# Who signals for TensorE: a drain behind each group of matmuls in place of the group's last matmul

## What is computed

```python
src, tgt = x[row], x[col]
h = relu(concatenate([src, tgt, edge_attr], -1) @ W1 + b1)
msg = h @ W2 + b2
attn = sigmoid(concatenate([msg, conf], -1) @ Wa + ba)
out = segment_sum(msg * attn, col, num_segments=100000)
return layernorm(x + out)
```

## Time and profile before

| | us |
|---|---|
| median of the 3 runs shown | 793.27 |
| lowest, highest | 778.97, 797.54 |
| profiled execution, from its first to its last instruction (span) | 792.5 |
| PE matmuls busy | 425.7 |
| DVE busy | 502.9 |
| ACT busy | 427.9 |
| POOL busy | 457.6 |

### The profile page before, as it was taken

The page is one execution under the profiler, slowest core; times in us unless marked ns, Lnnn a source line. Parts: engine busy times, 40 slices in busy tenths (PEclk is TensorE's granted clock), DMA queues, the critical chain, the costliest instruction groups (busy, mean ns, idle before and its releaser), DMA issues. The chain is left out here.

```text
span 792.5 us, 8991 instructions
## 1 busy us (share of the span) xinstructions
PE 425.7 (54%) x1902; PEld 299.8 (38%) x1902; DVE 502.9 (63%) x2146; ACT 427.9 (54%) x1089; POOL 457.6 (58%) x473
## 2 busy tenths in 40 slices
PE   1842778463764136763646566656463475543560
PEld 0531545332543123643435254444251254322250
DVE  5944988878793228883667579888461995330542
ACT  0433686678963047691546567757641698520360
POOL 7676572665666756464755735575746366467330
PEclk9985988777786558985887767977866889776785
DMA  7946678888886226685576568886754657431120
GB/s 190 357 133 208 224 273 299 279 293 254 268 305 207 84 82 219 241 297 171 173 241 199 184 221 264 291 281 232 253 160 133 234 159 233 117 116 59 35 59 14
DMA packets 79882, 159.37 MB, mean 201 GB/s; under 512 B 13970, under 2 KB 48086, under 8 KB 79826
## 3 DMA queue, kind: packets, MB, share of 16 engines
q1 hardware_dynamic: 65106, 129.47, 48.8%
q0 software_dynamic: 14720, 29.32, 13.1%
HBM read 99.75 MB, written 59.95 MB: 202 GB/s over the span
## 5 line engine op out<-in xcount | busy, mean ns | idle before, releaser
L887 PE MATMUL hid_ps<-turned,w 128*128 128x512 f32 x294 | 184.1, 776 | 102.4 <-issue 52.8
L741 ACT ACTIVATE turned<-turn_ps 128x512 f32<-128x512 f32 x147 | 80.3, 590 | 193.5 <-remote 130.0
L760 ACT ACTIVATE nodes<-nodes,sc 128x128 f32<-128x128 f32 (+1 forms) x462 | 184.0, 485 | 0.0
L641 POOL DMA_INDIRECT rows_src<-x,src_list x132 | 131.8, 998 | 85.4 <-issue 36.9
L662 POOL DMA_INDIRECT out<-stash,row_idx x132 | 131.3, 994 | 75.8 <-issue 40.2
L652 POOL DMA_INDIRECT rows_dst<-x,dst_list x132 | 125.8, 953 | 82.8 <-issue 36.2
L1186 DVE BATCH_NORM_STATS2 stats<-nodes 128x6 f32<-128x128 f32 (+1 forms) x693 | 152.8, 278 | 7.7 <-DMA nodes<-x 5.7
L887 PEld LDWEIGHTS hid_ps<-turned,w 128*128 128x128 f32 x294 | 69.6, 253 | 179.7 <-issue 126.5
L921 PE MATMUL sum_ps<-gated,place 128*128 128x128 f32 x384 | 69.1, 342 | 113.6 <-DVE near L1313 62.2
L897 PE MATMUL msg_ps<-w2x,hid 128*128 128x129 f32 x392 | 69.1, 331 | 108.0 <-ACT hid L746 71.4
L921 PEld LDWEIGHTS sum_ps<-gated,place 128*128 128x128 f32 x384 | 60.7, 241 | 131.5 <-DVE near L1313 65.8
(11 more groups left out here) (146 smaller groups left out, 510.1 us busy)
## 6 DMA issues: line engine op xcount, KB each, us to landing
nodes<-x SPq DMA_DIRECT2D x62, 704.0 KB
out<-nodes SPq DMA_DIRECT2D x62, 704.0 KB
attr_in<-edge_attr SPq DMA_DIRECT2D x49, 256.0 KB
near_dst<-line SPq DMA_DIRECT2D x16, 256.0 KB
near_x<-x SPq DMA_DIRECT2D x20, 192.0 KB
near_x<-x SPq DMA_DIRECT2D x24, 128.0 KB
out<-near SPq DMA_DIRECT2D x4, 704.0 KB
rows_src<-x,src_list POOLq DMA_INDIRECT x132
```

The costliest lines, as they stand in the source:

```text
L641: pool.indirect_dma_start(out=rows_src[:, k % RING, j, :], out_offset=None, in_=x[:, :], in_offset=bass.IndirectOffsetOnAxis(ap=idx[:, j:j ...
L741: act.activation(turned[:, k % 2, c], turn_ps[:, c], ACT.Copy).then_inc(turned_ready, 1)
L760: return act.activation(row, row, ACT.Identity, scale=sc[0:parts, b % 2, 0, col:col + 1], bias=sc[0:parts, b % 2, 1, col:col + 1])
L887: last = pe.matmul(hid_ps[:], w1[:, c, :], turned[:, k % 2, c, :], start=(c == 0), stop=(c == 2))
```

## The change

Every place of PE's loop where the last matmul of a group carried the signal now has a drain of PE behind the group, and the drain carries the signal. A drain is an instruction of the engine's sequencer that is over when the work given to the engine before it is. The order of the groups, the waits, the semaphores and their counts stay the same. The matmuls before the loop and those in `general()` (for unsorted inputs, not run here) keep their signals.

```diff
@@ turn(k)
                 for j in range(G):
-                    last = pe.transpose(turn_ps[:, 0, j * P:(j + 1) * P], rows_src[:, s, j, :], ident[:])
-                last.then_inc(turned_ps_ready, 1)
+                    pe.transpose(turn_ps[:, 0, j * P:(j + 1) * P], rows_src[:, s, j, :], ident[:])
+                pe.drain().then_inc(turned_ps_ready, 1)
...
@@ hidden(k)
                 for c in range(3):
-                    last = pe.matmul(hid_ps[:], w1[:, c, :], turned[:, k % 2, c, :], start=(c == 0), stop=(c == 2))
-                last.then_inc(hid_ps_ready, 1)
+                    pe.matmul(hid_ps[:], w1[:, c, :], turned[:, k % 2, c, :], start=(c == 0), stop=(c == 2))
+                pe.drain().then_inc(hid_ps_ready, 1)
@@ messages(k)
-                last.then_inc(msg_ready, 1)
+                pe.drain().then_inc(msg_ready, 1)
@@ sum_near(k), once for each of its four groups
-                    last.then_inc(sum_ready, 1)
+                    pe.drain().then_inc(sum_ready, 1)
@@ sum_v, sum_tail, sum_head
-                pe.matmul(sum_ps[:, use % 2, 0:F], v_match[:], head[0:1, 0, :], start=True, stop=True
-                          ).then_inc(sum_ready, 1)
+                pe.matmul(sum_ps[:, use % 2, 0:F], v_match[:], head[0:1, 0, :], start=True, stop=True)
+                pe.drain().then_inc(sum_ready, 1)
```

More of the change, by code:

```diff
@@ L865, in turn @@
                     for j in range(G):
-                        last = pe.transpose(turn_ps[:, 1, j * P:(j + 1) * P], rows_dst[:, i % RING, j, :], ident[:])
+                        pe.transpose(turn_ps[:, 1, j * P:(j + 1) * P], rows_dst[:, i % RING, j, :], ident[:])
                 else:
@@ L874, in turn @@
                             b = first + j * width + w
-                            last = pe.matmul(turn_ps[:, 1, j * P:(j + 1) * P], near_x[:, b, :],
+                            pe.matmul(turn_ps[:, 1, j * P:(j + 1) * P], near_x[:, b, :],
                                              pick[:, b * P:(b + 1) * P], start=(w == 0), stop=(w == width - 1))
-                last.then_inc(turned_ps_ready, 1)
+                pe.drain().then_inc(turned_ps_ready, 1)
                 pe.wait_ge(attr_landed[s], 16 * (k // RING + 1))
                 for j in range(G):
-                    last = pe.transpose(turn_ps[:, 2, j * P:(j + 1) * P], attr_in[:, s, j, :], ident[:])
-                last.then_inc(turned_ps_ready, 1)
+                    pe.transpose(turn_ps[:, 2, j * P:(j + 1) * P], attr_in[:, s, j, :], ident[:])
+                pe.drain().then_inc(turned_ps_ready, 1)
             def hidden(k):
@@ L896, in messages @@
                 for j in range(G):
-                    last = pe.matmul(msg(j), hid[:, k % 2, j * P:(j + 1) * P], w2x[:], start=True, stop=True)
-                last.then_inc(msg_ready, 1)
+                    pe.matmul(msg(j), hid[:, k % 2, j * P:(j + 1) * P], w2x[:], start=True, stop=True)
+                pe.drain().then_inc(msg_ready, 1)
             def bank_free(use):
@@ L920, in sum_near @@
                         b = first + j * width + w
-                        last = pe.matmul(sum_ps[:, use % 2, w * P:(w + 1) * P], place[:, b * P:(b + 1) * P],
+                        pe.matmul(sum_ps[:, use % 2, w * P:(w + 1) * P], place[:, b * P:(b + 1) * P],
                                          gated[:, k % 2, j, :], start=True, stop=True)
-                    last.then_inc(sum_ready, 1)
+                    pe.drain().then_inc(sum_ready, 1)
             def sum_v():
@@ L937, in sum_tail @@
                 pe.wait_ge(tail_saved, l)
-                pe.matmul(sum_ps[:, use % 2, 0:F], corner[:], tail[:, l - 1, :], start=True, stop=True
-                          ).then_inc(sum_ready, 1)
+                pe.matmul(sum_ps[:, use % 2, 0:F], corner[:], tail[:, l - 1, :], start=True, stop=True)
+                pe.drain().then_inc(sum_ready, 1)
             def sum_head(l):
@@ L945, in sum_head @@
                 pe.wait_ge(head_ready, HEAD_T * (l + 1))
-                pe.matmul(sum_ps[:, use % 2, 0:F], shift[:], head[:, l % 2, :], start=True, stop=True
-                          ).then_inc(sum_ready, 1)
+                pe.matmul(sum_ps[:, use % 2, 0:F], shift[:], head[:, l % 2, :], start=True, stop=True)
+                pe.drain().then_inc(sum_ready, 1)
             turn(0)
```

## The result

The changed kernel took 827.95 us (median of 4, 822.17 to 837.48), the kernel before 792.59 beside it (4 runs, 778.97 to 797.54): ratio 1.0645, 95% interval [1.0511, 1.0778]. Ratios with an interval leave out the slower executions of a kernel; the medians of all runs give 1.045 here, 35.4 us. The forecast was 697. The first rival (837) had the direction and nearly the size.

A forecast was written before the change was run, and what follows sets the result against it. It took PE's late signals to hold the other engines, with POOL the next bound. Of 792.5 us, 0.8 x 132.4 of POOL's waits would go and 10 be added: 696.6, so 697 us; likeliest case 660 to 745, wide range 655 to 840.

The forecast's parts named there:

- The first rival: PE's drains come as late as the matmuls' signals did, so the wait moves into PE: 837 us, chance 0.24.
- What bounds the kernel: PE's late signals hold ACT and DVE (288.1 us of waits, partly at once); POOL has the least slack.
- the sum (792.5 - 0.8 x 132.4 + 10): Whole span: less four fifths of POOL's 132.4 us of waits for other engines, plus 10 for drains: 696.6 us.
- the 48.5 us of waiting for DMAs: POOL's list of waits: eight kinds of waits for DMAs to land, 48.5 us in all, left as they were.
- I take the signal as prompt: PE's drains: their signals come promptly, for a gain of up to 132.4 us; chance hardly over one half.
- The rival's price, 44 us: First rival's loss on PE: 29 us of waits plus 15 of lost overlap, 792.5 + 44 = 837; chance 0.24.
- the held groups, 29 us: PE's next hidden group pushed by the messages' 1.28 us at each of 23 late waits: 29 us.
- 15 us of lost overlap: Part of the first rival: 15 of the 104 us of overlap that PE loses to drains.
- The mark set for the rival: PE's stalls: drains of over 0.5 us there would decide for the first rival (chance 0.24).
- the first sign of being wrong: Trace of the changed kernel: PE drains of several us would show the forecast wrong.
- Cost of a drain: Behind each of 315 PE groups: about 0.33 us of lost overlap, 104 us in all, 10 charged.
- The rival "signals stay as late, behind a sequencer that goes on", 803: PE's signals: same waits as before, plus 10 us of lost overlap, 803 us; chance 0.17.

The follow-up runs named there:

- D: Late session on chip 7: kernel before 807.9 us; a silent drain behind each group, signals left on the last matmuls, took 879.7, 1.089 by the medians.
- e4b: Kernel before with 0.2 to 0.33 us of further matmuls per group and no drain, late session: 830.0 us against 805.1, 1.031 by the medians.
- B: Session on chip 7 without late ends: kernel before 692.9 us; the changed kernel run again took 695.7, ratio 1.003 [0.998, 1.008].
- e4: Kernel before with 0.2 to 0.33 us of further matmuls per group and no drain, session without late ends: 692.7 us, ratio 0.998 [0.993, 1.004].
- g1_no_gathers: Changed kernel with memsets for all but the first 24 of GpSimd's indirect DMAs, late session: 698.1 us, 0.882 [0.863, 0.900] of the kernel before.
- the stretches: Separate kernel: eight stretches of 48 transpose groups beside different loads, drains except in the eighth; 396.1, 357.3, 354.0 us in prompt sessions, 446.4 in the late one.
- C: Session on chip 3 without late ends, kernel before unchanged: median 695.6 us (691.0 to 699.0).
- E: Session on chip 15 with many late ends, kernel before unchanged: median 805.1 us (788.2 to 827.5).

## Why the prediction was wrong

**What bounds the kernel: right.** Late signals of TensorE held ACT, DVE and POOL. In four sessions without them the kernel before takes 693 to 696 us; the prediction had 697 for a kernel rid of them, from POOL's list of waits. That the sum (792.5 - 0.8 x 132.4 + 10) comes out so near is in part luck. In the prompt trace of the changed kernel nearly all of the 132.4 us are gone, not four fifths, and the 48.5 us of waiting for DMAs, which it left as they were, are 93. These two errors, 25 and 44 us, work against each other. And the change is not what removes the late signals.

**"I take the signal as prompt": the step that failed.** Its reason was that "what was late in the earlier trace rows was not the work, since PE took three more groups meanwhile, but the signals that the matmuls carried". That TensorE takes new groups shows only that its queue goes on. Whether a group has ended, as the engine counts it, a matmul's end in the trace can't say (it is modelled), and the drain does: 17.5 us at L877, 212 us of lateness in all. The silent drains (D) settle it, since there the matmuls still carry the signals, and the drains without one are late together with them, within 1.4 us. By the Trainium skill (PSUM — Partial Sum Buffer, Engine vs sequencer instructions) a drain waits until the engine is fully idle; the trace agrees, with "idle" taking in what makes the signal late. The price of being wrong was the whole distance from 697 to 828.

**The rival's price, 44 us: nearly right** (measured 35.4 by the medians, 51 by the ratio). It lay in the held groups, 29 us, and 15 us of lost overlap. That groups are held is shown: PE, which never stood idle ahead of L880 in the kernel before, does so for 15.66 us behind a drain and for 54.2 us in all, and POOL's waits for L861 grew from 68.7 to 104.0 us for L862. The size of 23 x 1.28 us is not shown, and how the two parts share the loss isn't settled; e4b puts up to 25 us (830.0 - 805.1) on lost overlap, in overlapping ranges. PE's busy time rose from 425.7 to 496.6 us for the same matmuls; the granted clock fell from 0.77 to 0.751 as well, so that part of this rise is not the drains' own. The mark set for the rival, drains of over 0.5 us standing in the stalls, was met, and so was the first sign of being wrong, drains of several us; 0.5 us was set too low, though, for the median drain behind a group in prompt sessions is 0.63 us.

**Cost of a drain, 0.33 us of lost overlap each and 10 us charged of 104: right in kind.** It ends 0.02 us after the last matmul. In the changed kernel the groups of transposes start 0.73 us apart where 0.44 stood in the earlier trace rows, so 0.29 us. In a prompt session (B) 315 of them cost 2 us (1.003 of 692.9, interval -2 to 6), hidden beside waits for gathers, as e4 shows with work in their place.

**The rival "signals stay as late, behind a sequencer that goes on", 803:** refuted by the timeline at 666 to 682 us, where the queue stands.

## What makes the ends late: how far it is settled

Shown: they go with indirect DMAs of GpSimd in quick succession, in some sessions only; with memsets in the place of all but the first 24 there are none. Not shown: what differs between sessions.

One observation narrows it. The trace also records updates of semaphores, and an indirect DMA makes 16 of them. In the two late traces of the changed kernel there are 5,383 and 5,358 such records, in the prompt one 14,142; in `g1_no_gathers`, in a late session, 7,033, of some 7,600 that it makes by that count. In the stretches it can be seen where they are missing:

| stretch | updates made by gathers | recorded, prompt (C) | recorded, late (E) | late drains (E) |
|---|---|---|---|---|
| 2, back to back | 448 | 448 | 84 | 8 |
| 3, one at a time | 448 | 448 | 448 | 0 |
| 7, back to back, with transfers | 448 | 437 | 48 | 6 |
| 8, back to back, with ScalarE | 448 | 448 | 79 | no drains; late signals |

In the stretches records are missing in number exactly where ends are late, and not those of gathers alone: in stretch 7 of E, 24 of 128 updates of SyncE's transfers are recorded (128 in C). But `g1_no_gathers` lacks records without late ends: of the 384 updates of its 24 indirect DMAs 117 are recorded, and no drain is late there. So missing records alone don't make an end late. A reading that still fits is that in late sessions the path on which such records leave can't keep up with 16 updates each 1.25 us, and, when that lasts, holds TensorE's completions back. By the Trainium skill (NOTIFIC — the notification-queue block, 7.1 Overflow: three behaviours, one of which stalls the engine) the block that writes records throttles its producers inside rather than lose records there; no run here shows that block at work, and that rule would give held-back records, not missing ones. The rival reading, that something slows updates themselves and records are lost as a consequence, is as open. Every execution of this study was recorded in this way, so whether the late level exists without recording isn't known either. No run gives the gathers fewer updates in a late session, or leaves the recording out; these would help to tell the two apart.

## What to carry to other kernels

A matmul's end in a profile is modelled. Where a reader of PSUM starts long after it, don't conclude that the work is done and only its signal late: put one silent drain behind the group and see how long it lasts. Where ends can be late, each drain turns the lateness of a signal, which the queue could pass by, into a stop of the whole queue; where they are prompt, a drain costs its group's overlap (0.29 us here), which is nothing so long as the engine waits elsewhere. And before a stall is treated as the kernel's own, run the unchanged kernel in other sessions: here the 100 us that the change aimed at were not there in four of seven.

## What the runs showed that I had not expected

- Two levels of one kernel, 693 and 808 us, on the same chip (7) in two sessions.
- Ends of matmuls up to 10 us late beside GpSimd's gathers at one each 1.25 us (up to 19.7 us in the kernels), and none late at one each 2.75 us, with as many gathers.
- A drain right behind a drain takes 13 ns.
- Silent drains made the kernel faster by 1.7% [1.0, 2.4] in one prompt session, by 1.2% [-0.3, 2.6] in another.
- With memsets on GpSimd at the place of indirect DMAs, DVE's busy time for the same 2,146 instructions was 589.7 us, not 505.0 (500.6 in the prompt trace with the DMAs).
